# Mixer B: where the next pair's exponents stand among the input projection's blocks and the diagonal products

## The reference, cut to what matters

```python
proj = hidden_states @ in_proj_w * _mup_vector()
z, xBC, dt = ...                                    # 1024, 1024 + 2 * 128, 64 columns
xBC = silu(conv4(xBC) + conv_b);  x, Bm, Cm = ...   # depthwise, 4 taps, causal
dt = softplus(dt + dt_bias);  dA = exp(-exp(A_log) * dt)
state = state * dA[t] + outer(dt[t] * x[t], B[t])   # per head, t = 0 .. 1023
y[t] = C[t] @ state + D * x[t]
out = (y * rsqrt(mean(y * y) + eps) * norm_w * silu(z)) @ out_proj_w
```

## Time and profile before

| what | value |
|---|---|
| median of three runs | 2862.99 us (2861.88 to 2865.03) |
| profiled execution, first to last instruction | 2859.7 us |
| PE busy | 2733.3 us, 96% of the span |
| DVE busy | 2009.9 us, 70% |
| ACT busy | 1527.0 us, 53% |
| POOL busy | 926.1 us, 32% |
| mean granted TensorE clock | 0.980 |
| mixer B, 1381 to 2620 us: PE, DVE, ACT, POOL busy | 1213.1, 1032.0, 854.0, 457.7 us of 1239.0 |

### The profile page before, as it was taken

One profiled execution on the slowest core, in us unless ns is written; L12 is line 12 of the kernel. 1 busy time (PEld: TensorE's weight loads), 2 busy tenths in 40 slices (PEclk: granted clock), 3 DMA queues, 4 the chain that ended last, 5 costly groups with the idle time before them and its releaser, 6 DMA issues. The chain is left out here.

```text
span 2859.7 us, 49906 instructions
## 1 busy us (share of the span) xinstructions
PE 2733.3 (96%) x17464; PEld 1845.0 (65%) x17464; DVE 2009.9 (70%) x3695; ACT 1527.0 (53%) x2418; POOL 926.1 (32%) x614
## 2 busy tenths in 40 slices
PE   7999999999999999996899999999999999997996
PEld 6777766777766665455666666666666666664453
DVE  5666666666666663377788888888888888885267
ACT  3444444445455442341577666766667776665242
POOL 2222223222223321232233444333333334332134
PEclk9999999999999999998999999999999999998998
DMA  4000000000000034145000000000000000022333
GB/s 125 23 23 22 22 22 22 23 28 29 22 22 22 16 121 152 45 147 204 12 23 22 22 22 16 21 22 22 15 15 22 22 22 22 15 95 89 112 118 133
DMA packets 79935, 139.59 MB, mean 49 GB/s; under 512 B 17896, under 2 KB 17896, under 8 KB 78832
## 3 DMA queue, kind: packets, MB, share of 16 engines
q1 hardware_dynamic: 70752, 125.92, 12.9%
q10 hardware_dynamic: 9104, 12.63, 1.4%
HBM read 104.98 MB, written 33.55 MB: 48 GB/s over the span
## 5 line engine op out<-in xcount | busy, mean ns | idle before, releaser
L655 PE MATMUL work<-b_xnT,shared_w 128*128 128x256 f32 x2304 | 545.8, 388 | 1.8 <-DVE b_parts L1192 1.3
L655 PE MATMUL work<-a_xnT,shared_w 128*128 128x256 f32 x2176 | 509.4, 392 | 1.3
L655 PEld LDWEIGHTS work<-b_xnT,shared_w 128*128 128x128 f32 x2304 | 426.1, 191 | 90.6 <-issue 30.1
L655 PEld LDWEIGHTS work<-a_xnT,shared_w 128*128 128x128 f32 x2176 | 419.0, 195 | 73.8 <-issue 12.3
L1232 DVE TENSOR_TENSOR b_decay<-b_decay,b_gt 128x1024 f32<-128x1024 f32 x256 | 351.7, 1395 | 119.3 <-ACT b_decay L943 115.8
L936 ACT ACTIVATE b_decay<-seg 128x1024 f32<-128x1024 f32 x256 | 248.5, 1029 | 112.0 <-PE seg L781 111.8
L943 ACT ACTIVATE b_decay<-b_decay 128x1024 f32<-128x1024 f32 x256 | 266.1, 1073 | 0.0
L1406 POOL TENSOR_TENSOR b_rhs<-b_l_side,of_head 128x1024 fp32r<-128x1024 f32 x32 | 82.0, 2563 | 552.4 <-DVE b_l_side L1201 552.4
L1441 POOL TENSOR_TENSOR a_y<-a_y,a_skip 128x1024 f32<-128x1024 f32 x32 | 90.9, 2840 | 484.1 <-DVE a_y L1221 484.1
L1111 DVE SCALAR_TENSOR_TENSOR shared_cv<-shared_pre,a_conv_w,shared_cv 128x256 f32<-128x256 f32 x432 | 189.7, 482 | 74.6 <-ACT shared_cv L880 68.9
L1111 DVE SCALAR_TENSOR_TENSOR shared_cv<-shared_pre,b_conv_w,shared_cv 128x256 f32<-128x256 f32 x480 | 232.1, 517 | 14.2 <-ACT shared_cv L880 6.3
(11 more groups left out here) (314 smaller groups left out, 4612.4 us busy)
## 6 DMA issues: line engine op xcount, KB each, us to landing
shared_x<-in_L_attn_a_x SPq DMA_DIRECT2D x16, 512.0 KB, 3.5
a_x_res<-in_L_attn_a_x SPq DMA_DIRECT2D x32, 256.0 KB, 2.6
x_mid<-a_x_res SPq DMA_DIRECT2D x32, 256.0 KB, 2.1
shared_w<-in_L_ffn_d_w SPq DMA_DIRECT2D x2, 4096.0 KB, 14.0
f_d_w<-in_L_ffn_d_w SPq DMA_DIRECT2D x2, 4096.0 KB, 14.5
f_x_res<-x_mid SPq DMA_DIRECT2D x8, 1024.0 KB, 5.9
f_bc_w<-x_mid SPq DMA_DIRECT2D x8, 1024.0 KB, 5.6
shared_x<-x_mid SPq DMA_DIRECT2D x16, 512.0 KB, 3.6
```

What stands on the lines that cost most here:

```text
L655: mm = nc.tensor.matmul(dst, w_in[:, k, col:col + m], xnT[:, k, :], start=(k == 0), stop=(k == KD - 1))
```

## The change

In both halves the exponents of pair p + 1 now stand directly in front of the diagonal products of pair p. In half 0 they stood between that pair's two runs of blocks. In half 1 the eight transposes that add y1 to the y bank (`ident1`, L815) stood behind the first such unit and now stand ahead of it. ACT and DVE follow: the next pair's Relu, exponentials and multiplications come one place of blocks later than before, the second exponential behind the first run of blocks of the next pair.

```diff
@@ schedule (PE)
             for p in range(NP):
-                steps += fill0[2 * p] if nxt else []
-                steps += [f"seg0.{p + 1}"] if p + 1 < NP else []
-                steps += fill0[2 * p + 1] if nxt else []
+                steps += fill0[2 * p] + fill0[2 * p + 1] if nxt else []
                 if p + 1 == NP:
                     steps += state_steps(0)
+                steps += [f"seg0.{p + 1}"] if p + 1 < NP else []
                 steps += [f"ydiag0.{2 * p}", f"ydiag0.{2 * p + 1}"]
...
             for p in range(NP):
                 steps += fill1[2 * p] if nxt else []
+                if p == 0 and NP > 1:
+                    steps += ["ident1"]
                 steps += [f"seg1.{p + 1}"] if p + 1 < NP else (["sums"] if nxt else [])
                 steps += fill1[2 * p + 1] if nxt else []
                 if p + 1 == NP:
                     steps += (["small0"] if nxt else []) + state_steps(1)
-                if p == 0:
+                if NP == 1:
                     steps += ["ident1"]
                 steps += [f"ydiag1.{2 * p}", f"ydiag1.{2 * p + 1}"]
@@ supertile (ACT), half 0
                     for p in range(NP):
-                        behind = fill0[2 * p + 1] if nxt else []
+                        if p:
+                            slot_bound(sec, 0, 2 * p)
+                            slot_bound(sec, 0, 2 * p + 1)
+                            slot_exp(sec, 0, 2 * p)
                         if nxt:
                             fills(sec, fill0[2 * p])
-                        if p + 1 < NP:
-                            slot_bound(sec, 0, 2 * p + 2)
-                            slot_bound(sec, 0, 2 * p + 3)
-                            slot_exp(sec, 0, 2 * p + 2)
-                            fills(sec, behind[:1])
-                            slot_exp(sec, 0, 2 * p + 3)
-                            fills(sec, behind[1:])
-                        else:
-                            fills(sec, behind)
+                        if p:
+                            slot_exp(sec, 0, 2 * p + 1)
+                        if nxt:
+                            fills(sec, fill0[2 * p + 1])
@@ supertile (DVE), half 0
                     for p in range(NP):
+                        if p:
+                            slot_mult(sec, 0, 2 * p)
+                            slot_mult(sec, 0, 2 * p + 1)
                         for g in (2 * p, 2 * p + 1):
...
-                            if g % 2 == 0 and p + 1 < NP:
-                                slot_mult(sec, 0, 2 * p + 2)
-                                slot_mult(sec, 0, 2 * p + 3)
-                            elif g % 2 == 0:
+                            if g % 2 == 0 and p + 1 == NP:
                                 exponent_sides(2 * i + 1)
```

## The result

The changed kernel takes 2894.41 us (median of 4 runs, 2893.4 to 2895.91), the kernel before 2863.17 (4 runs, 2861.88 to 2865.03): a ratio of 1.0109, 95% interval 1.0095 to 1.0123. It is slower by 31.2 us; 35.2 were forecast. The profiled executions are 2892.1 and 2859.7 us from first to last instruction, 32.4 apart.

A forecast was written before the change was run, and what follows sets the result against it. PE was taken to bound mixer B, busy 78.20 of 78.65 us. 15 x 1.42 = 21.3 us for half 0 plus 16 x 0.87 = 13.9 for half 1 gave 35.2 us, median 2898.2, range 2884 to 2914.

The forecast's parts named there:

- Half 1: Mixer B, second half: transposes no longer cover ACT's two Relus, so the second exponents start 0.87 us later in 16 supertiles.
- Half 0: Mixer B, first half: DVE's longer pauses reach PE whole, 1.42 us in each of 15 supertiles.
- For the two later pairs DVE is so far behind that their exponentials are there in time: Half 0, slots 4 to 7: exponentials ready before DVE's multiplications, with margin 0.3 us at slot 7.
- what follows comes 1.4 us later: Half 0 on DVE: pauses of 3.45 us in place of 2.01 delay state_add and the square sums, taken as 1.42.
- all one lateness of DVE: Half 0: PE's waits at slot 3 (0.6 us), z0a (1.0) and yoff1b are not added up, +1.42 at yoff1b.
- From 2030.49 on it works without a break: Half 0, kernel before: DVE has no pause from 2030.49 until the copy of the square sums at 2055.50.
- B: Rival: DVE's lateness in half 0 is hidden and PE's own list decides there; +4.9 us, 2868; 5 in 100.
- C: Rival: PE's list alone sets the end in both halves, so faster; -10.6 us, 2852; 3 in 100.
- sum for the saved switches: Half 0 on PE: the new order saves 0.20 us three times per supertile, 0.6; no gain while DVE sets the end.
- D: Rival: ACT's second exponential is late for later pairs too, each adding 0.5 to 1 us; +58 us, 2921; 8 in 100.
- A: Rival: PE's clock falls to half for 4 us once per supertile, losing 2 us each; +67 us, 2930; 6 in 100.
- a lone one: Last supertile, earlier trace: a wait of 1.01 us came alone and the exponents behind it kept their 0.51.

The follow-up runs named there:

- the other DVE list: New half 0 order, state_add and gate directly behind block 7, taps of blocks 8, 9 behind output addition; second exponential behind whole first run 2861.51 us, behind first block 2852.19.
- the last run: Kernel before with only DVE's list changed: state_add and gate directly behind block 7, taps of blocks 8 and 9 behind the output tile's addition; 2859.52 us.
- the first of the last three: Kernel before with new half 0 order, second exponential behind first block, state_add and gate behind block 7, taps of blocks 8, 9 behind output addition; 2852.19 us.

## Why the prediction was right, and where its reason was not

**Half 1: right, term for term.** 0.87 forecast, 0.86 measured alone, with a wait of 1.02 on ACT for the forecast 1.1. Sixteen of them are 13.8 us; the run with that edit alone is 12.3 up by its medians.

**Half 0: the size nearly, the mechanism half.** Worked forward, PE's part came out within 0.06: `seg0.1` 3.55 forecast and 3.61 measured behind dt, `seg0.2` 10.38 and 10.43. The pauses before slots 2 and 3 were forecast at 1.3 and 2.1 and are 1.25 and 1.97. The term itself was 1.42, and is 1.10.

The step that did not hold as worked out is "For the two later pairs DVE is so far behind that their exponentials are there in time", and with it that "what follows comes 1.4 us later". The exponentials were there in time, but the margin of slot 7, put at 0.3, is 0.04. In the new order the last pair's exponents start at 17.86 behind dt, and from there Relus, exponential 6, block 7, exponential 7 and its multiplication, block 7's taps and the exponent sides lead to `state_add` 9.8 later, however little DVE carries ahead of slot 7: 27.65. With the second exponential earlier the exponents start at 17.26 and `state_add` is at 27.03. So the 1.10 has two parts. 0.61 goes with the place of the second exponential (79.75 against 79.13, and 78.80 against 78.19 with the other DVE list): behind the whole run it delays both DVE and, through PE's wait of 0.60 at the diagonal product of slot 3, the last pair's exponents. The remaining 0.48 is there with the exponential moved forward, too, where it is the last pair's chain up to the bank that z0a needs. The run with less DVE work separates this from my reading: a backlog alone would have given its 0.8 us back, and nothing came. I had written that these waits are all one lateness of DVE. For z0a and `yoff1b` that holds; but the first wait, at slot 3, is one of its causes and not its sign.

The size was off for a second reason as well. "From 2030.49 on it works without a break" was read from merged rows. Two multiplications without a wait take 2.35 us in the changed kernel. In the kernel before, the row of slots 4 and 5 begins at 2035.69 and the next one at 2038.20, 2.51 later; in the changed kernel the distance is 2055.56 to 2057.83, 2.27. So the kernel before had small pauses in there, too short to be listed, of 0.24 and, by the same reckoning, of some 0.15 for slots 6 and 7 (from the rows 2041.07 and 2043.50, 2.43 apart): there, too, DVE waits a little for exponentials 5 and 7. The new order took them away, and 1.42 less these 0.4 is about what was measured.

**What made up the rest.** 15 x 1.10 + 16 x 0.87 = 30.4 us. Measured are 31.2 on the medians, 32.4 on the spans. On the profiled span the one long period adds 2.5 (83.26 less 78.83, less the usual 1.96); what comes before mixer B was 1.2 shorter in that execution and what comes behind its last exponents 1.1 longer, though nothing is changed in either. That gives 32.8. What comes before mixer B differs by up to 6.3 us between the profiled executions, so a single span is no measure of an effect of this size.

**The rivals.** B and C needed DVE's pauses to be harmless, and did not come. Their sum for the saved switches was right, though: the gain of 0.54 a supertile between the last run and the first of the last three is the 0.6 of the prediction, and it appears once DVE's list makes room. D, a wait for each later pair, did not show in the changed kernel, but was nearer the truth than my 8 in 100: slot 7 stood 0.04 us from it, and with the second exponential moved forward the waits for slots 5 and 7 appear, 0.32 and 0.40. A, the clock, did not come. In the loop it stayed at 1.00 with waits of 0.39, 0.56, 0.41 and 1.01 us in 80.6, so the rule of the Trainium skill (TensorE: Matmul & The Clock Gate, "A second HAM failure mode") is not borne out at this density. The clock stands at 0.50 in the last supertile, and the wait of 1.01 in the earlier trace rows, which the prediction calls a lone one, is the first of several there, in both kernels:

```profile
2578.51 0.64 PE L795 MATMUL y<-b_decay,b_xdt 128*32 128x128 f32 x16 [1.60 <-DVE b_decay L1232]
2579.64 1.08 PE L795 MATMUL y<-b_decay,b_xdt 128*32 128x128 f32 x16 [0.49 <-DVE b_decay L1232]
```

That these waits brought the clock down fits the order of events, but no run tests it.

**Not settled.** DVE and POOL collide over the exponent sides in every period. Why DVE loses in half 0 of the second period of the changed kernel, and wins in the others of the loop, was not tried; the distance of their records, 0.16 us, is the same in both cases.

## What to carry to other kernels

Before moving a producer towards its consumer, write down for each of its uses what covers the engines between, one pair after the other and the last pair too: eight transposes of 0.87 us were the whole cover of two Relus here. When several waits stand on one engine, take work from that engine before calling them a backlog; if the time does not move, a chain from another engine ends no earlier than the backlog, and the pauses only shift. Note where the work was taken from: only what stands ahead of the meeting point is tested. A saving of switches on the engine that sets the time is worth having only after the other engine's list has been changed to deliver in time: the same 0.5 us a supertile came first with a loss of 1.1 for the whole edit of half 0, and then with a gain of 0.46 a period (0.4% of the kernel by the medians), with the second exponential and the state's sum moved forward.

## What the runs showed of the hardware

When DVE and POOL work at the same time, almost the whole cost can fall on one of them. Six taps on DVE took 2.80 us almost alone, 3.85 partly beside POOL, and 8.06 beside POOL instructions of 6.8 us together, which themselves took 2.35, 2.47 and 1.99 us (in the kernel before, beside other DVE work, 2.35, 3.09 and 2.80). In that run a tap ended 0.28 to 0.29 us behind each end of a POOL instruction, so DVE got one tap through for each. The 3.85 is made the same way: its first tap takes 1.62 and ends 0.28 behind POOL's instruction.

The two exponent sides, DVE's and POOL's, run at the same time and end in one of two ways: DVE's takes 1.22 and POOL's 3.13, or DVE's 2.92 and POOL's 2.00. POOL's record begins 0.16 us ahead in either case, so the records don't say what decides. In half 0 of the loop DVE is the faster in the kernel before and in the changed one; in the run of 2852.19 us it is the slower in every half.

This agrees with the Trainium skill (GPSIMD Engine Reference, "Specifications"), by which the two share the interface to SBUF and VectorE instructions with two inputs there contend with GpSimd. How the cost falls, one side nearly all of it, is this trace's.

A switch of PE costs 0.10 us from the projection's blocks to the exponents and 0.20 from the blocks to the diagonal products (in the trace of the kernel before a single block ahead of them takes 1.93, of which 1.73 are the block). Merging three runs of blocks saved 0.54 a supertile, the difference between the last run and the first of the last three.
